# Fused last attention stage: maxima taken off transposed scores in PSUM by TensorE, output bias by a three-row bf16 matmul

## What is computed

```python
qn = _layer_norm(query, ln1_g, ln1_b); kn = _layer_norm(key, ln1_g, ln1_b); vn = _layer_norm(value, ln1_g, ln1_b)
Q = (qn @ wq + bq).reshape(B, Sq, H, HD)      # K, V the same from kn, vn
scores = jnp.einsum('bqhd,bkhd->bhqk', Q, K) / jnp.sqrt(jnp.float32(HD))
attn = jax.nn.softmax(scores, axis=-1)
out = jnp.einsum('bhqk,bkhd->bqhd', attn, V).reshape(B, Sq, E) @ wo + bo
x = residual + out
return x + (gelu(_layer_norm(x, ln2_g, ln2_b) @ w1 + b1) @ w2 + b2)
```

## Time and profile before

| | |
|---|---|
| time of three executions | 1389.43, 1391.83, 1393.59 us, median 1391.83 |
| the profiled execution | 1399.14 us, its span 1397.3 us |
| fused stage, first scores to last normalise | 964.4 to 1263 us |
| mean granted TensorE clock | 0.967 |

### The profile page before, as it was taken

The page is one execution under the profiler, slowest core; times in us unless marked ns, Lnnn a source line. Parts: engine busy times, 40 slices in busy tenths (PEclk is TensorE's granted clock), DMA queues, the critical chain, the costliest instruction groups (busy, mean ns, idle before and its releaser), DMA issues. The chain is left out here.

```text
span 1397.3 us, 59862 instructions
## 1 busy us (share of the span) xinstructions
PE 1242.1 (89%) x23050; PEld 1031.0 (74%) x23050; DVE 953.1 (68%) x2152; ACT 988.4 (71%) x1972; POOL 899.7 (64%) x1432
## 2 busy tenths in 40 slices
PE   4999999989999998958999999985878788788997
PEld 2777877777878887837999999953666666665775
DVE  3888888876787886594555555546889999854331
ACT  1778777767888887346787776624988888865553
POOL 2577777776677665216999998767677777413331
PEclk9999999999999999579999999997999999999999
DMA  4233343322222220051222222243222222112221
GB/s 125 77 108 117 110 126 106 114 86 86 83 82 83 82 76 26 16 136 39 69 65 68 66 67 67 66 143 103 63 68 68 73 73 73 41 49 61 68 74 39
DMA packets 137984, 109.81 MB, mean 79 GB/s; under 512 B 16928, under 2 KB 113696, under 8 KB 137888
## 3 DMA queue, kind: packets, MB, share of 16 engines
q1 hardware_dynamic: 129440, 91.22, 22.1%
q0 software_dynamic: 8448, 17.32, 5.2%
HBM read 74.35 MB, written 34.08 MB: 78 GB/s over the span
## 5 line engine op out<-in xcount | busy, mean ns | idle before, releaser
L907 DVE TENSOR_REDUCE at_mx<-at_ps_s 128x16 f32<-128x1024 f32 x128 | 156.0, 1220 | 91.9 <-PE at_ps_s L587 47.2
L813 ACT ACTIVATE at_pt<-at_ps_t 128x1024 f32<-128x1024 f32 x128 | 130.6, 1020 | 55.3 <-PE at_ps_t L608 54.5
L2357 POOL DMA_INDIRECT ex_xg<-x,ex_ti x136 | 146.3, 1076 | 23.5 <-issue 21.9
L806 ACT ACTIVATE at_pr<-at_dd 128x1024 f32<-128x1024 f32 x128 | 135.2, 1056 | 34.7 <-DVE at_dd L915 34.6
L2471 DVE COPY ex_wt<-experts 128x1156 f32 x133 | 102.7, 772 | 80.4 <-DVE ex_y L2477 74.4
L2429 ACT ACTIVATE ex_hg<-ex_ps_h,ex_wt 128x128 f32<-128x128 f32 x544 | 154.6, 374 | 1.2 <-PE ex_ps_y L2388 1.2
L915 DVE TENSOR_TENSOR at_dd<-at_ps_s,at_mx 128x1024 f32<-128x1024 f32 x128 | 153.7, 1202 | 0.1
L2379 PE MATMUL ex_ps_h<-ex_xt,ex_wt 128*128 128x128 f32 x1088 | 146.5, 278 | 1.0 <-ACT ex_xt L2421 0.8
L2016 POOL DMA_INDIRECT l_yg<-rows,l_sl x128 | 125.8, 983 | 31.9 <-issue 29.4
L608 PE MATMUL at_ps_t<-ident,at_pr 128*128 128x128 f32 x1024 | 140.0, 280 | 6.0 <-issue 5.4
L2388 PE MATMUL ex_ps_y<-ex_wt,ex_hg 128*128 128x128 f32 x1088 | 143.6, 275 | 0.4 <-ACT ex_hg L2429 0.4
(11 more groups left out here) (264 smaller groups left out, 3166.5 us busy)
## 6 DMA issues: line engine op xcount, KB each, us to landing
rows<-ex_y SPq DMA_DIRECT2D x136, 64.0 KB
x<-at_ln_out SPq DMA_DIRECT2D x32, 256.0 KB, 3.2
at_kx<-in_xt SPq DMA_DIRECT2D x16, 256.0 KB, 2.8
at_qx<-in_xt SPq DMA_DIRECT2D x16, 256.0 KB, 2.8
at_vin<-in_xt SPq DMA_DIRECT2D x16, 256.0 KB, 2.8
at_xr<-in_x SPq DMA_DIRECT2D x16, 256.0 KB, 3.0
cx<-in_ctx SPq DMA_DIRECT2D x16, 256.0 KB, 3.2
x1t<-at_xt SPq DMA_DIRECT2D x16, 256.0 KB, 3.3
```

What stands on the lines that cost most here:

```text
L806: act.activation(pr[:, p], dd[:, p], ACT.Exp, scale=SCALE).then_inc(p_ready, 1)
L813: act.activation(pt[:, 2 * h + p], ps_t[:, :, :, :], ACT.Copy).then_inc(pt_ready, 1)
L907: dve.tensor_reduce(mx[:, p], ps_s[:, :, 4 * p:4 * p + 4, :], AX.X, ALU.max).then_inc(mx_ready, 1)
L2357: pool.indirect_dma_start(out=xg[:, s, :], out_offset=None, in_=x_src, in_offset=bass.IndirectOffsetOnAxis(ap=ti[:, s:s + 1], axis=0)).the ...
```

## The change

- The scores are computed twice. `scores(a, i)` now makes one quarter: eight matmuls with queries as rows, into `ps_s` (two banks), for the maxima alone, and, abreast of them on the other half of the array's rows, eight with keys as rows and queries as columns for the quarter before, into `ps_t` (two buffers of two banks). What `turn` produced is now produced directly, so `turn`, `subtract`, `copy_t` and the buffers `dd`, `pr` are gone.
- The maxima are subtracted in PSUM. DVE takes them (`maximum`) and splits each f32 into three bf16 parts with two small subtractions (`split`); PE turns them with one bf16 matmul (`turn_largest`), ACT copies the 64x128 result to SBUF as bf16 (`copy_largest`), and eight bf16 matmuls with -1 at the right places add minus the maxima to the transposed scores (`take_largest`). Then ACT takes the exponential straight from PSUM into `pt` (`exponent`).
- `turn_largest(n)` writes into the `ps_t` buffer of quarter n-1 and so waits for `exponent(n-1)`.
- The masked keys come by DMA: SP copies them from `x2t` into the places of `kb` that aren't zero, eight transfers of 16 partitions x 4 x 256 bytes for half a group, sixteen a step (`mask_k`, now on SP). The bias of K is added when the keys are projected.
- `mask_q` and `copy_v` work on halves of a group; `vin` has two buffers.
- The bias bo (with bv folded in) is split into three bf16 parts once; a matmul of three contraction rows starts `ps_g` with it and `project_out` adds on top. `add_bias` on POOL is gone and `residual` reads the held rows.
- All lists of the step are written anew. Values of groups 8 to 15 are staged in `x3` instead of `dd` and `pr`.

```diff
+                def mask_k(a, h):
+
+                    if a.unrolled and a.g == 0 and h == 0:
+                        sp.wait_ge(kt_ready, NG)
+                        sp.wait_ge(set_up, 2)
                     if beyond(a.g, 0):
-                        sp.wait_ge(vx_ready, a.g)
-                    sp.dma_start(vin[:, :], layer.kv_src[:, bass.ts(a.place, GT)]).then_inc(in_v, 16)
+                        sp.wait_ge(s_ready, 4 * a.g + 2 * h - 1)
+                    for j in range(2):
+                        for r in range(4):
+                            heads = slice(32 * r + 16 * j, 32 * r + 16 * j + 16)
+                            sp.dma_start(kb[heads, h, :, j, :],
+                                         zt[heads, bass.ds(a.place * GT + GT // 2 * h, GT // 2)].rearrange(
+                                             "p (b s) -> p b s", b=QB)).then_inc(in_k[h], 16)
...
+                def scores(a, i):
+
+                    n, h, rp = 4 * a.g + i, i // 2, i % 2
+                    before_h = h if rp == 1 else 1 - h
+                    own, last = a.exists(), i > 0 or a.shift(-1).exists()
+                    if own and rp == 0:
+                        pe.wait_ge(in_k[h], 16 * 8 * (a.g + 1))
...
                     for b in range(QB):
-                        t = SEQ * (QB * h + b)
-                        for r in range(4):
-                            rows = slice(32 * r, 32 * r + 32)
-                            mm = pe.matmul(ps_s[:, r, 2 * b:2 * b + 2, :], qb[rows, QB * h + b, :, :],
-                                           kb[rows, :, t:t + SEQ], start=(b == 0),
-                                           stop=(b == QB - 1 and not causal), skip_group_check=True)
...
+                        if own:
+                            for r in range(2):
+                                rows = slice(64 * rp + 32 * r, 64 * rp + 32 * r + 32)
+                                mm = pe.matmul(ps_s[:, r, 2 * b:2 * b + 2, :], qb[rows, h, b, :, :], kb[rows, h, b, :, :],
+                                               start=(b == 0), stop=(b == QB - 1), skip_group_check=True)
+                        if last:
+                            for r in range(2):
+                                rows = slice(64 - 64 * rp + 32 * r, 64 - 64 * rp + 32 * r + 32)
+                                mm = pe.matmul(ps_t[:, 1 - rp, r, b, :], kb[rows, before_h, b, :, :],
+                                               qb[rows, before_h, b, :, :], start=(b == 0), stop=False,
+                                               skip_group_check=True)
                     mm.then_inc(s_ready, 1)
-                def turn(quad, h, p):
-
-                    pair = quad * 2 + p
-                    pe.wait_ge(p_ready, pair + 1)
-                    if beyond(pair, 0):
-                        pe.wait_ge(pt_ready, pair)
-                    for b in range(2):
-                        for r in range(4):
-                            tr = pe.transpose(ps_t[:, b, r, :], pr[:, p, r, 2 * b:2 * b + 2, :], c.ident[:, :])
-                    tr.then_inc(t_ready, 1)
+                def turn_largest(a, i):
+
+                    n, rp = 4 * a.g + i, i % 2
+                    pe.wait_ge(parts_ready, n + 1)
+                    if beyond(n, 0):
+                        pe.wait_ge(pt_ready, n)
+                    pe.matmul(ps_t[:, 1 - rp, 0, 0, :], mx[:, rp, :].bitcast(BF16).rearrange("p (x t) -> p x t", t=2)[:, :, 1],
+                              same_b[:, :], start=True, stop=True).then_inc(mt_ready, 1)
+
+                def take_largest(a, i):
+
+                    n, rp = 4 * a.g + i, i % 2
+                    pe.wait_ge(mc_ready, n + 1)
+                    for b in range(QB):
+                        for r in range(2):
+                            rows = slice(64 * rp + 32 * r, 64 * rp + 32 * r + 32)
+                            mm = pe.matmul(ps_t[:, rp, r, b, :], minus[rows, b, :], mt[rows, :], start=False,
+                                           stop=(b == QB - 1), skip_group_check=True)
+                    mm.then_inc(t_ready, 1)
...
                 def project_out(a):
                     pe.wait_ge(ot_ready, 2 * a.g + 2)
+                    if beyond(a.g, 0):
+                        pe.wait_ge(y_ready, a.g)
+                    pe.matmul(ps_g[:, :], ones_b[0:3, :], bob_parts[0:3, :].bitcast(BF16).rearrange(
+                        "p (d t) -> p d t", t=2)[:, None, :, 1].broadcast_to([3, GP, D]), start=True, stop=False,
+                        skip_group_check=True)
                     for t in range(GP):
                         mm = pe.matmul(ps_g[:, D * t:D * t + D], ot[:, P * t:P * t + P], layer.wo[:, :],
-                                       start=True, stop=True)
+                                       start=False, stop=(t == GP - 1), skip_group_check=True)
                     mm.then_inc(o_ready, 1)
...
+                def exponent(a, i):
+
+                    n, h, rp = 4 * a.g + i, i // 2, i % 2
+                    if a.unrolled and n == 0:
+                        act.wait_ge(v_out, 16 * NG)
+                    act.wait_ge(t_ready, n + 1)
+                    if beyond(a.g, 0):
+                        act.wait_ge(pv_ready, 2 * a.g + h - 1)
+                    act.activation(pt[:, h, :, 2 * rp:2 * rp + 2, :].rearrange("p b r q -> p r b q"), ps_t[:, rp],
+                                   ACT.Exp, scale=SCALE).then_inc(pt_ready, 1)
+
+                def copy_largest(a, i):
+
+                    n, rp = 4 * a.g + i, i % 2
+                    half = slice(64 * rp, 64 * rp + 64)
+                    act.wait_ge(mt_ready, n + 1)
+                    if beyond(n, 1):
+                        act.wait_ge(t_ready, n - 1)
+                    act.activation(mt[half, :], ps_t[half, 1 - rp, 0, 0, :], ACT.Copy).then_inc(mc_ready, 1)
...
-                def subtract(quad, p):
-
-                    pair = quad * 2 + p
-                    dve.wait_ge(mx_ready, pair + 1)
-                    if beyond(pair, 1):
-                        dve.wait_ge(p_ready, pair - 1)
-                    dve.tensor_tensor(dd[:, p], ps_s[:, :, 4 * p:4 * p + 4, :],
-                                      mx[:, p, :, :, None].broadcast_to([P, 4, 4, SEQ]),
-                                      ALU.subtract).then_inc(d_ready, 1)
+                def maximum(a, i):
+                    n, rp = 4 * a.g + i, i % 2
+                    dve.wait_ge(s_ready, n + 1)
+                    if beyond(n, 1):
+                        dve.wait_ge(mt_ready, n - 1)
+                    dve.tensor_reduce(largest(rp, 0), ps_s[:, :, :, :], AX.X, ALU.max).then_inc(mx_ready, 1)
+
+                def split(a, i):
+
+                    n, rp = 4 * a.g + i, i % 2
+                    dve.wait_ge(mx_ready, n + 1)
+                    dve.tensor_tensor(largest(rp, 1), largest(rp, 0), high(rp, 0), ALU.subtract).then_inc(rest_ready, 1)
+                    dve.wait_ge(rest_ready, n + 1)
+                    dve.tensor_tensor(largest(rp, 2), largest(rp, 1), high(rp, 1), ALU.subtract).then_inc(parts_ready, 1)
...
-                def add_bias(a):
-                    if a.unrolled and a.g == 0:
-                        pool.wait_ge(bob_ready, 1)
-                    pool.wait_ge(x3_ready, a.g + 1)
-                    if beyond(a.g, 1):
-                        pool.wait_ge(y_ready, a.g - 1)
-                    pool.tensor_tensor(xb[:, a.u], held(a), bob[:, 0, None, :].broadcast_to([P, GP, D]),
-                                       ALU.add).then_inc(xb_ready, 1)
```

More of the change, by code:

```diff
@@ L1710, in mask_q @@
-                def mask_q(a):
+                    act.activation(zt[:, bass.ts(g, GT)], bank[g % 2][:, :], ACT.Identity, bias=layer.bk[:, 0:1]).then_inc(
+                        kt_ready, 1)
+                def mask_q(a, h):
+                    if a.unrolled and a.g == 0 and h == 0:
+                        act.wait_ge(set_up, 2)
                     act.wait_ge(q_ready, a.g + 1)
                     if beyond(a.g, 0):
-                        act.wait_ge(s_ready, 2 * a.g)
+                        act.wait_ge(s_ready, 4 * a.g + 2 * h - 1)
@@ L1787, in step @@
                     if a.shift(-1).exists():
[L1788 to L1791 removed]
+                        exponent(a.shift(-1), 2)
+                        copy_largest(a.shift(-1), 3)
+                        copy_o(g * 2 - 2, 0)
+                    if a.exists():
+                        copy_v(a, 0)
+                        mask_q(a, 1)
+                    if a.shift(-1).exists():
+                        exponent(a.shift(-1), 3)
+                    if a.exists():
+                        copy_largest(a, 0)
                     if a.shift(1).exists():
@@ L1809, in step @@
                     if a.shift(1).exists():
-                        mask_k(a.shift(1))
+                        copy_z(a.shift(1))
+                    if a.shift(2).exists():
+                        scale_own(a.shift(2))
                     if a.exists():
```

(10 more changed lines are left out.)

306 lines of the change are left out of this document (139 added, 167 removed).

## The result

The changed kernel takes 1487.8 us (median of 4 runs, 1484.2 to 1491.6) against 1392.3: a ratio of 1.069, 95% interval 1.066 to 1.072. Forecast were 1393 us, in a range of 1379 to 1410. Its profiled execution, the longest of the four, spans 1489.8 us, that of the kernel before 1397.3.

A forecast was written before the change was run, and what follows sets the result against it. The prediction took a ring of waits through DVE, POOL's root, ACT's scalings and PE to bound the kernel. Start, ramp, steady steps and tail summed to +0.8 us, giving 1393 us against 1391.8, range 1379 to 1410.

The forecast's parts named there:

- The new ring: A step's four exponentials in one chain, each turn of maxima waiting for the exponential before: 18.20 us a step.
- `values` occupies PE 2.0: In the walked chain of exponentials, each half group's values matmuls take 2.0 us on PE.
- The links without a row: Between exponentials: turn until ACT can start 0.30 us, copy 0.22, subtraction 0.55, handover 0.08; not all backed by profile rows.
- The work: Busy time a step: DVE 13.5 us, ACT 11.9, PE 14.7, POOL less 1.28; work alone would give about 16.
- Keys by DMA: Sixteen SP transfers a step; eight, spaced 0.55 us, need 6.2 us with landing and have 7.0, so hidden.
- the rival: Keys land late at the scores of quarters 0 and 2: 20.6 us a step, about 1426 us, chance 0.12.
- The check by a walk of the old lists: The same walk through the kernel before closed at 18.15 us against 18.06 measured, so the new figure was trusted.
- Start: Up to the first scores: half-group masks save 2.0 us, DVE's extra setup adds 0.5.
- Ramp: From the end of the key masks to group 0's second normalise: 31.6 us instead of 36.2, taken as -4.5.
- steady: Eleven steady steps, each 0.14 us longer than before: +1.5 us.
- tail: The last four groups, where front work ends and the new chain saves only about 5 us: +5.3 us.
- four cases: As walked (1389 to 1396 us) 0.37; shorter links (about 1383) 0.29; longer links (about 1405) 0.22; late keys 0.12.

The follow-up runs named there:

- Run 1: The changed kernel with VectorE's weigh_first moved from ahead of the first normalise to directly ahead of weigh_second: 1441.8 us, ratio 1.036.
- run 2: The changed kernel with GpSimd's last three gathers issued ahead of the reciprocal root: 1453.1 us, ratio 1.042.
- run 3: The changed kernel with an unused 1.27 us addition on GpSimd directly ahead of the last three gathers: 1511.4 us, ratio 1.087.
- run 6: The changed kernel with the last three of eight gathers left out, output not the reference's: 1436.6 us, ratio 1.031.
- run 8: The changed kernel with five of eight gathers and six unused matmuls on TensorE ahead of values(., 1): 1426.7 us, ratio 1.023.
- runs 10 and 12: The changed kernel with eight operations moved, gathers earlier, 1418.0 us; the changed kernel in another order of all engines, keys still by DMA, 1433.4 us.
- runs 15 and 16: The kernel before: with an unused GpSimd addition ahead of the last three gathers, 1410.9 us; with five of eight gathers, 1389.7 us.

## Why the prediction was wrong

- **"The new ring", the step that failed.** The walk was made over one ring and left out `weigh_first`'s wait for the gathers. The change moved the first normalise from the end of VectorE's list to directly behind `weigh_first`. On GpSimd it put `spread(0)` ahead of the root and the last three gathers, and `spread(1)`, which waits for the values, ahead of all five others, where three had stood ahead of it. That closed a ring of 24.04 us which was in no rival. Run 1 opens it (20.65), run 2 shortens it (21.74), run 3 doses it (+1.40), run 6 removes it (20.48): 3.56 us a step.
- **"`values` occupies PE 2.0".** A term of the sum that was mis-sized twice: 3.5 us where TensorE had waited (half clock), 2.8 to 3.3 where the keys are transferred. In the ring without gathers that is 1.0 us a step each in the mean, 2.0 of 20.5; 18.5 is left, as with the clock restored (run 8), and ScalarE's pieces behind exponential 2, 0.45 over what was taken, account for the rest. The prediction said that a clock under 1.00 would make PE's time wrong, and gave that no price and no chance.
- **The links without a row** were the stated main risk, and were right: turn to copy 0.25 to 0.35 us after the turn's start (0.30 + 0.08 taken), copy 0.27 (0.22), subtraction to exponential 0.44 (0.55 + 0.08). The 293 ns that the prediction estimates for that copy from the Trainium skill (ScalarE: Activation LUTs, What ACT_TABLE_LOAD costs, where the page has these figures) is 22 ns over the measured 271.
- **The work.** VectorE and GpSimd fell as counted, to 13.8 us a step (13.5) and 12.9 (13.0); ScalarE fell to 12.9 and not to 11.9; TensorE came to 16.7 for 14.7, part of it by the lower clock. That less work would not shorten the step was right; but GpSimd's stood on the ring that set it (run 3), and the walk had none of it.
- **Keys by DMA.** Right that they are hidden in this kernel, whose step leaves them more room than the one walked, with the wrong spacing: eight issues took 5.88 us, 0.73 each, not 0.55. What was missed is that the values beside them get longer, and that they are the next limit (runs 10 and 12). In the rival a lateness of 2.0 us (9.0 less 7.0) was written as 20.6 us a step; it gives 20.2 and about 1421 us. Nothing hangs on it.
- **The check by a walk of the old lists** (18.15 for 18.06) misled: it agreed while the rings of that kernel were of nearly the same length (as runs 15 and 16 suggest), so it tested the costs and not whether every dependence was there.
- **The sum.** Start -1.5 (-2.0 and +0.5), measured +7.4: GpSimd waited 11.6 us for the gain of the first group, whose operations stand later in the new lists. Ramp -4.5, measured +10.2; steady +1.5, measured +63.3 (the eleven steps before took 200.3 us, 18.21 each and not 18.06, so at 18.20 the forecast was 0 here); tail +5.3, measured +10.7.
- **The chances.** All ten in ten lay on four cases, and none of the four held a wait on a gather or a lower clock. The slower case with one mechanism, late keys, was a real limit, but of other orders of the lists (runs 10 and 12).

## What to carry to other kernels

When a change rewrites the lists of several engines, list for every operation that blocks an in-order queue (a wait on a DMA above all) who stands behind it now, and follow each of these until it comes back to itself; a walk over the ring that the change is about finds only that ring. An operation that is late at no cost today (a weighted sum behind a gather) must not stand ahead of one that others wait for. And a new wait on TensorE is to be priced with its clock: what followed a wait of some 4 us ran at half clock here, and cheap matmuls in the wait took it back.
